# Totals over partitions on PE instead of POOL, and the tail's bias row added by PE

## The reference

```python
x = x + L0_xattn(layernorm(x), ctx)   # causal self attention + cross attention, 16 heads of 16
x = x + L0_ffn(layernorm(x))          # per-token int8 input, weights rounded to -1, 0, 1
x = x + L1_xattn(layernorm(x), ctx)   # cross attention
x = x + L1_ffn(layernorm(x))          # one int8 scale for the whole tensor

def weight_quant(w):                  # L0_ffn: sum over the whole weight
    scale = 1.0 / clip(mean(abs(w)), 1e-5)
    return clip(round(w * scale), -1, 1) / scale

def quant_per_tensor(x):              # L1_ffn: maximum over the whole tensor
    scale = maximum(max(abs(x)), 1e-6) / 127
    return round(x / scale), scale

def qlinear(x, w, b):                 # L1_ffn, twice, with gelu between
    xq, sx = quant_per_tensor(x); wq, sw = quant_per_tensor(w)
    return (xq @ wq.T + b) * (sw * sx)
```

## Time and profile before

| | |
|---|---|
| median of three runs | 2048.04 us |
| the profiled execution | 2049.73 us |
| its span, first to last instruction | 2047.9 us |
| mean granted TensorE clock | 0.911 |
| PE busy | 1735.0 us (85%) |
| DVE busy | 1348.7 us (66%) |
| ACT busy | 1168.0 us (57%) |
| POOL busy | 739.7 us (36%) |
| POOL's partition reduces | 6 |

### The profile page before, as it was taken

How to read it: one execution, slowest core, us unless ns; L and a number is a source line. 1 busy time by engine, 2 the same in 40 slices (tenths; PEclk the granted TensorE clock), 3 DMA queues, 4 the chain that set the end, 5 groups by cost and what they waited for, 6 DMA issues and landing times.

```text
span 2047.9 us, 34236 instructions
## 1 busy us (share of the span) xinstructions
PE 1735.0 (85%) x10004; PEld 745.0 (36%) x10016; DVE 1348.7 (66%) x2478; ACT 1168.0 (57%) x2178; POOL 739.7 (36%) x984
## 2 busy tenths in 40 slices
PE   5897889987999889987999799987999798777676
PEld 1243334422443244432543244332442243231225
DVE  6567666777667666757677756766677757617378
ACT  1364475566655485556655585557555675552486
POOL 3322525541544126521544136521544042150034
PEclk7798889998999989987999999988999899786898
DMA  7224313232232313331232313222331223005023
GB/s 204 81 77 122 83 32 89 78 90 62 64 104 59 94 48 85 87 81 52 68 100 70 83 48 102 74 77 59 90 87 55 65 56 101 1 26 161 23 81 103
DMA packets 106988, 159.93 MB, mean 78 GB/s; under 512 B 20657, under 2 KB 83249, under 8 KB 106801
## 3 DMA queue, kind: packets, MB, share of 16 engines
q1 hardware_dynamic: 101904, 156.43, 27.7%
q10 hardware_dynamic: 4896, 1.18, 0.3%
HBM read 105.00 MB, written 51.38 MB: 76 GB/s over the span
## 4 chain that ended last, share of the span: by engine, by line
PE 56%; DVE 14%; issue 11%; ACT 8%; POOL 7%; DMA 2%; SPq 1%; ACTq 1%; DVEq 0%; POOLq 0%
PE acc L1390 13%; PE mx L1355 12%; PE st L1376 10%; DVE nmax L1176 8%; PE misc L1330 6%; PE misc L1302 3%; PE misc L1342 3%; PE misc L1417 3%; ACT probs L931 2%; PE misc L1444 2%; POOL qk L823 1%; DMA stack<-parts_fk 1%; POOL parts L825 1%; POOL parts L821 1%; POOL parts L827 1%
## 5 line engine op out<-in xcount | busy, mean ns | idle before, releaser
L1176 DVE TENSOR_REDUCE nmax<-mx 128x1 f32<-128x512 f32 (+2 forms) x1376 | 881.4, 674 | 458.0 <-PE mx L1355 276.7
L931 ACT ACTIVATE probs<-st 128x512 f32<-128x512 f32 (+3 forms) x1536 | 773.7, 548 | 516.1 <-PE st L1376 346.4
L1355 PE MATMUL mx<-stack 96*128 96x512 bf16 (+3 forms) x1536 | 574.3, 385 | 128.7 <-DVE nmax L1176 80.6
L1376 PE MATMUL st<-stack 99*128 99x512 bf16 (+3 forms) x1536 | 565.8, 378 | 68.6 <-ACT probs L931 57.6
L1376 PEld LDWEIGHTS st<-stack 99*128 99x128 bf16 x1536 | 152.0, 100 | 443.9 <-ACT probs L931 262.2
L1355 PEld LDWEIGHTS mx<-stack 96*128 96x128 bf16 x1536 | 154.6, 101 | 342.9 <-DVE nmax L1176 237.4
L821 POOL TENSOR_TENSOR parts<-qk,zero 128x512 bf16<-128x512 f32 x94 | 98.1, 1043 | 302.5 <-ACT qk L914 302.5
L833 POOL TENSOR_TENSOR nparts<-nmax,zero 128x16 bf16<-128x16 f32 x96 | 21.1, 220 | 405.4 <-DVE nmax L1176 398.2
L1390 PE MATMUL acc<-probs,v_x 128*32 128x512 f32 x1024 | 151.0, 665 | 0.0
L1390 PE MATMUL acc<-probs,v_f 128*32 128x512 f32 x1024 | 147.4, 650 | 0.4 <-ACT probs L931 0.3
L1379 PE MATMUL st<-mask_st,identb 128*128 128x128 bf16 x512 | 112.2, 222 | 0.0
(11 more groups left out here) (231 smaller groups left out, 2051.5 us busy)
## 6 DMA issues: line engine op xcount, KB each, us to landing
parts_xk<-parts SPq DMA_DIRECT2D x48, 128.0 KB
parts_xq<-parts SPq DMA_DIRECT2D x48, 128.0 KB
stack<-parts_xq SPq DMA_DIRECT2D x32, 192.0 KB, 3.1
stack<-parts_xk SPq DMA_DIRECT2D x32, 192.0 KB, 3.7
parts_sk<-parts SPq DMA_DIRECT2D x48, 128.0 KB
parts_sq<-parts SPq DMA_DIRECT2D x48, 128.0 KB
stack<-parts_sq SPq DMA_DIRECT2D x32, 192.0 KB, 2.9
stack<-parts_sk SPq DMA_DIRECT2D x32, 192.0 KB, 3.5
```

What stands on the lines that cost most here:

```text
L931: act.activation(probs[:, j % P_SLOTS, c, T - w:], st_bank(n, 4 * j + c)[:, 0:w], ACT.Exp, scale=SCALE).then_inc(exp_done, 1)
L1176: dve.tensor_reduce(nmax[:, ring, first:first + NT * (len(cs) - 1) + 1:NT], src, AX.X, ALU.max, negate=True).then_inc(mx_free, 1)
L1355: last = pe.matmul(o, stack[0:ROWS, r, 0, c, P * i:P * i + P], stack[0:ROWS, r, 1, c, 0:w], start=True, stop=not causal)
L1376: last = pe.matmul(o[:, 0:w], stack[0:AUG, r, 1, c, P * j:P * j + P], stack[0:AUG, r, 0, c, T - w:T], start=True, stop=not causal)
```

## The change

The six `partition_all_reduce` of POOL go. For n = 0 and 1 PE multiplies wsum with a 128 x 128 view of a column of ones, which leaves the sum in every partition (`w_tot`). For the four maxima PE transposes the column into a row of one partition (`w_row`; in the tail `t_tot` and `t_htot`), DVE reduces the row to one number, and PE multiplies it with a row of ones (`to_all`); DVE reads the total from PSUM. In the order of steps the empty card and `w_scale` become `w_tot`, and for n = 2 and 3 two more cards come in, so the later cards of that list move by up to one or two places. PE now waits for DVE's `w_sum` in its own order at these steps.

In the tail POOL no longer adds G2. PE opens each of its four accumulations of a batch with an f32 matmul of the row of ones against the unscaled row G2 (256 columns), and hscale1 scales it together with the product; DVE's `sums` waits for the residual's load itself. L1242 goes, and ACT starts at `t_hsc` 3 instead of 4. After its last quantising POOL does nothing. One memset (`ones1`) is new at the start. Left out of the diff below are declarations, semaphores and the tables of steps.

```diff
@@ -216,7 +214,7 @@
-            [("w_peak", n), None, None, ("w_scale", n), ("w_ints", n, 0), None, ("w_ints", n, 1), None, ("w_ints", n, 2)] +
+            [("w_peak", n), None] + [("w_row", n), None] * (n >= 2) + [("w_tot", n), None, ("w_ints", n, 0), None, ("w_ints", n, 1), None, ("w_ints", n, 2)] +
@@ -256,7 +254,7 @@
-    "misc": {"weights": 1, "ctx_T": 1, "norm_T": 2, "project": 1, "v": 2, "negmax_T": 1, "heads_out": 1,
+    "misc": {"weights": 1, "w_row": 1, "w_tot": 1, "ctx_T": 1, "norm_T": 2, "project": 1, "v": 2, "negmax_T": 1, "heads_out": 1,
@@ -748,6 +746,7 @@
+            pool.memset(ones1[:, :], 1.0).then_inc(consts_made, 1)
@@ -768,11 +767,6 @@
-            def w_peak(s):
-                n = s.b.base
-                pool.wait_ge(w_sum, n + 1)
-                pool.partition_all_reduce(wtot[:, n, :], wsum[:, n, :], P, RADD if n < 2 else RMAX).then_inc(w_tot, 1)
@@ -858,12 +852,10 @@
-            pool.wait_ge(peak, 2 * B)
-            pool.partition_all_reduce(xtot[:, :], xrun[:, :], P, RMAX).then_inc(t_tot, 1)
@@ -874,13 +866,6 @@
-            pool.wait_ge(t_hsc, 1)
-            pool.partition_all_reduce(htot[:, :], hrun1[:, :], P, RMAX).then_inc(t_htot, 1)
-            pool.wait_ge(t_hsc, 5)
-            for n in range(B):
-                pool.wait_ge(t_res[n], 16)
-                add_row(tail_res[n].rearrange("p (t c) -> p t c", c=C), Bv["G2"], t_bias)
@@ -994,7 +979,7 @@
-            act.wait_ge(t_hsc, 4)
+            act.wait_ge(t_hsc, 3)
@@ -1035,15 +1020,18 @@
-            def w_scale_(s):
-                n = s.b.base
-                dve.wait_ge(w_tot, n + 1)
-                if n < 2:
-                    dve.tensor_scalar(wscale[:, n, :], wtot[:, n, :], 1.0 / (F * C), 1e-5, ALU.mult, ALU.max).then_inc(w_scale, 1)
-                else:
-                    dve.tensor_scalar(wscale[:, n, :], wtot[:, n, :], 1e-6, 1.0 / QP, ALU.max, ALU.mult).then_inc(w_scale, 1)
-                dve.wait_ge(w_scale, 2 * n + 1)
+            def w_row(s):
+                slot = misc_slot(s)
+                wait_misc_full(dve, s)
+                dve.tensor_reduce(wrow[:, :], misc[slot][0:1, 0:P], AX.X, ALU.max).then_inc(misc_free[slot], 1)
+            def w_tot(s):
+                n, slot = s.b.base, misc_slot(s)
+                wait_misc_full(dve, s)
+                limits = (1.0 / (F * C), 1e-5, ALU.mult, ALU.max) if n < 2 else (1e-6, 1.0 / QP, ALU.max, ALU.mult)
+                dve.tensor_scalar(wscale[:, n, :], misc[slot][:, 0:1], *limits).then_inc(misc_free[slot], 1)
+                wait_misc_read(dve, s)
@@ -1051,7 +1039,7 @@
-                    dve.wait_ge(w_scale, 2 * n + 2)
+                    dve.wait_ge(w_scale, n + 1)
@@ -1210,13 +1198,15 @@
-            dve.tensor_scalar(xscale[:, :], xtot[:, :], 1e-6, 1.0 / QP, ALU.max, ALU.mult).then_inc(t_sc, 1)
+            dve.tensor_reduce(trow[:, 0:1], mx[0][0:1, 0:P], AX.X, ALU.max).then_inc(t_row, 1)
+            dve.wait_ge(t_tot, 2)
+            dve.tensor_scalar(xscale[:, :], mx[1][:, 0:1], 1e-6, 1.0 / QP, ALU.max, ALU.mult).then_inc(t_sc, 1)
@@ -1234,12 +1224,13 @@
-            dve.tensor_scalar(hscale[:, :], htot[:, :], 1e-6, 1.0 / QP, ALU.max, ALU.mult).then_inc(t_hsc, 1)
+            dve.tensor_reduce(trow[:, 1:2], misc[0][0:1, 0:P], AX.X, ALU.max).then_inc(t_row, 1)
+            dve.wait_ge(t_htot, 2)
+            dve.tensor_scalar(hscale[:, :], misc[1][:, 0:1], 1e-6, 1.0 / QP, ALU.max, ALU.mult).then_inc(t_hsc, 1)
...
-            dve.tensor_scalar(Bv["G2"][:, :], Bv["G2"][:, :], hscale1[:, :], None, ALU.mult).then_inc(t_hsc, 1)
@@ -1252,7 +1243,7 @@
-                dve.wait_ge(t_bias, n + 1)
+                dve.wait_ge(t_res[n], 16)
@@ -1293,6 +1284,26 @@
+            def w_row(s):
+                pe.wait_ge(w_sum, s.b.base + 1)
+                wait_misc_free(pe, s)
+                pe.transpose(misc[misc_slot(s)][0:1, 0:P], wsum[:, s.b.base, :], ident[:, :]).then_inc(misc_full, 1)
+            def w_tot(s):
+                n, o = s.b.base, misc[misc_slot(s)][:, 0:1]
+                if n < 2:
+                    pe.wait_ge(w_sum, n + 1)
+                    wait_misc_free(pe, s)
+                    pe.matmul(o, ones1[:, :].to_broadcast([P, P]), wsum[:, n, :], start=True, stop=True).then_inc(misc_full, 1)
+                else:
+                    wait_misc(pe, s, 0, [misc_read(s, 0, ("w_row", n))])
+                    to_all(o, wrow[:, :]).then_inc(misc_full, 1)
+            def to_all(o, value):
+                return pe.matmul(o, ones1[0:1, :].to_broadcast([1, P]), value, start=True, stop=True)
@@ -1480,11 +1491,16 @@
+                        o = out_pairs[n % 2][h][:, C * t:C * t + C]
+                        pe.matmul(o, ones1[0:1, :].to_broadcast([1, P]), Bv["G2"][0:1, :], start=True, stop=False)
...
-                            last = pe.matmul(out_pairs[n % 2][h][:, C * t:C * t + C], tail_hq[:, n % 2, f, first:first + P],
-                                             w2T[:, f, :], start=f == 0, stop=f == KF - 1)
+                            last = pe.matmul(o, tail_hq[:, n % 2, f, first:first + P], w2T[:, f, :], start=False, stop=f == KF - 1)
...
+            pe.wait_ge(peak, 2 * B)
+            pe.transpose(mx[0][0:1, 0:P], xrun[:, :], ident[:, :]).then_inc(t_tot, 1)
+            pe.wait_ge(t_row, 1)
+            to_all(mx[1][:, 0:1], trow[:, 0:1]).then_inc(t_tot, 1)
@@ -1494,6 +1510,10 @@
+            pe.wait_ge(t_hsc, 1)
+            pe.transpose(misc[0][0:1, 0:P], hrun1[:, :], ident[:, :]).then_inc(t_htot, 1)
+            pe.wait_ge(t_row, 2)
+            to_all(misc[1][:, 0:1], trow[:, 1:2]).then_inc(t_htot, 1)
```

More of the change, by code:

```diff
@@ L33 @@
 AX = mybir.AxisListType
-RMAX = bass.bass_isa.ReduceOp.max
-RADD = bass.bass_isa.ReduceOp.add
 P = 128
@@ L420, in two_layers_kernel @@
         wsum = sb("wsum", [P, 4, 1])
-        wtot = sb("wtot", [P, 4, 1])
+        wrow, trow, ones1 = sb("wrow", [1, 1]), sb("trow", [1, 2]), sb("ones1", [P, 1])
         wscale = sb("wscale", [P, 4, 1])
         winv = sb("winv", [P, 4, 1])
-        xpeak, xrun, xtot, xscale, xinv = (sb(n, [P, 1]) for n in ("xpeak", "xrun", "xtot", "xscale", "xinv"))
-        hscale1, hrun1, htot, hscale, hinv, oscale = (sb(n, [P, 1]) for n in ("hscale1", "hrun1", "htot", "hscale", "hinv", "oscale"))
+        xpeak, xrun, xscale, xinv = (sb(n, [P, 1]) for n in ("xpeak", "xrun", "xscale", "xinv"))
+        hscale1, hrun1, hscale, hinv, oscale = (sb(n, [P, 1]) for n in ("hscale1", "hrun1", "hscale", "hinv", "oscale"))
         hpeak = sb("hpeak", [P, B // 2 * KF])
@@ L466, in two_layers_kernel @@
         NFIRST = 6
-        NMADE = 12
+        NMADE = 13
         consts_in, consts_made = sem("consts_in"), sem("consts_made")
@@ L493, in two_layers_kernel @@
         peak, stored = sem("peak"), sem("stored")
-        w_in, w_sum, w_tot, w_scale, w_quant, w_kept = \
-            (sem("ffn_w_" + n) for n in ("in", "sum", "tot", "scale", "quant", "kept"))
+        w_in, w_sum, w_scale, w_quant, w_kept = \
+            (sem("ffn_w_" + n) for n in ("in", "sum", "scale", "quant", "kept"))
         zeroed, waited = sem("zeroed"), sem("waited")
@@ L591, in two_layers_kernel @@
         t_turn, t_turned, t_peak, t_mag, t_round = sem("t_turn"), sem("t_turned"), sem("t_peak"), sem("t_mag"), sem("t_round")
-        t_out, t_sum, t_bias = sem("t_out"), sem("t_sum"), sem("t_bias")
-        t_hsc, t_htot, t_end = sem("t_hsc"), sem("t_htot"), sem("t_end")
+        t_out, t_sum = sem("t_out"), sem("t_sum")
+        t_row, t_hsc, t_htot, t_end = sem("t_row"), sem("t_hsc"), sem("t_htot"), sem("t_end")
         def st_bank(n, k):
@@ L859, in down_q @@
                 pool.tensor_tensor(hq[:, t % 2, :], hid[:, t, :], magic[:, :].to_broadcast([P, F]), ALU.subtract).then_inc(hq_full, 1)
-            walk(pool, dict(consts_rest=consts_rest, w_peak=w_peak, stats=stats_, norm=norm, mid_bias=mid_bias, project=project, negmax=negmax,
+            walk(pool, dict(consts_rest=consts_rest, stats=stats_, norm=norm, mid_bias=mid_bias, project=project, negmax=negmax,
                             y_T=y_T, hid_scale=hid_scale, down_q=down_q))
-            pool.wait_ge(peak, 2 * B)
-            pool.partition_all_reduce(xtot[:, :], xrun[:, :], P, RMAX).then_inc(t_tot, 1)
             pool.wait_ge(t_sc, 2)
@@ L1211, in finish @@
                 dve.tensor_tensor(xrun[:, :], xrun[:, :], xpeak[:, :], ALU.max).then_inc(peak, 1)
-            walk(dve, dict(consts=consts, consts_rest=consts_rest, project=project, w_peak=w_peak, w_scale=w_scale_, w_ints=w_ints, stats=stats_, norm=norm, x_scale=x_scale, quant_x=quant_x, hidden=hidden,
+            walk(dve, dict(consts=consts, consts_rest=consts_rest, project=project, w_peak=w_peak, w_row=w_row, w_tot=w_tot, w_ints=w_ints, stats=stats_, norm=norm, x_scale=x_scale, quant_x=quant_x, hidden=hidden,
                            hid_peak=hid_peak, hid_scale=hid_scale, down=down, v=v, maxima=maxima, heads_out=heads_out,
@@ L1445, in down @@
                 last.then_inc(misc_full, 1)
```

(2 more changed lines are left out.)

## The result

The changed kernel takes 2088.23 us (median of four runs, 2083.99 to 2089.55) against 2048.57 for the kernel before in the same session: ratio 1.0187, 95% interval 1.0169 to 1.0205. It is slower by 40 us, where 10.5 us less was forecast. The profiled execution took 2087.48, its span is 2085.4, so 37.5 more than the span before.

What follows compares the result with a forecast made beforehand. PE, busy 85% of the span, bounds the kernel through the batch loop, which the change leaves alone. Terms -16.0 - 2.5 + 6.0 + 0.4 + 1.6 = -10.5 us gave 2037.6 us, range 2029 to 2046.

Steps and rivals of the forecast that it cites:

- Last pass: Tail's final pass: bias matmuls make PE the bound at 5.51 us a batch, +1.6 us.
- rival C: Last pass: PE's clock does not come up; slower by over 4 us, all eight batches give +30; chance 0.08.
- First turn: First turn of the walk: removing four POOL reduces and their silent times, less added waits, gives -16 us.
- my four units: The four first-turn units that turn a weight into integers: together -21 us before added waits.
- x1: First unit with a weight in the first turn: from 25.05 to 17 us, -8.
- x2: Second unit with a weight in the first turn: down to 14.5 us, -5.9.
- s1: Third unit with a weight in the first turn: down to 15.5 us, -4.
- s2: Fourth unit with a weight in the first turn: down to 18 us, -3.
- those for the DMA: First turn: weights' loads lose cover, so DVE waits for them; +2.2 us.
- rival B: First turn: PE's waits for DVE's sums replace the stall; gain only 6, total -0.5 us; chance 0.15.
- Hand-over: Walk to tail: total over PE comes sooner, -2.5 us; POOL beside DVE stretches DVE's four instructions, +6.
- The step from hrun to hscale: In the tail: the reduce cost DVE only 0.55 us, the chain over PE 0.95; +0.4.

Runs made afterwards that it cites:

- the entry warm: Changed kernel plus 18 unused bf16 matmuls of 512 columns ahead of the last pass, so PE enters at full clock: 2041.13 us, pass 61.6.
- the run with the first turn alone: Kernel before with the totals of the four weights by PE, tail unchanged: 2033.32 us against 2050.16, ratio 0.993.
- the run with the hand-over alone: Kernel before with only the maximum over x taken across partitions by PE instead of POOL: 2048.85 us in one run.
- the waiting POOL: Changed kernel with a 128-row bf16 bias, POOL quantising batch 2 only after DVE rounded batches 0 and 1: 2023.99 us against 2050.16, ratio 0.987.
- the bias edited: Kernel before with the bias by PE as a one-row f32 matmul, no add_row, all six reduces still on POOL: 2109.73 us, pass 104.6.

## Why the prediction was wrong, step by step

**Last pass: the step that failed.** I wrote that "PE needs 3.67 + 1.84 = 5.51 a batch", with both durations read at clock 1.00, and let the low clock cost "a little" in the first batch. That the clock comes up was an assumption, taken from a pass in which it did. The engine's mixture was what the change altered. I gave rival C, where it stays low, only 0.08, because "now PE has none" of the idle times: but it was not idleness that kept the clock down here, since PE has none in 94 us. What did was the one-row matmuls: without them, or with 64 or 128 rows in their place, the clock rises. Two errors add up:

- The clock: 104.5 us against 61.6 with the entry warm, 43 of the 51 us.
- The price of a one-row matmul. I read 0.46 from a form with 128 rows, and 128 rows cost 0.43 here. One row costs 0.73 at full clock, and so do 64: before their weight loads PE's load queue stands idle at full clock too (26 loads with 64 rows: 2.7 us in all, "issue"), where before those of 128 rows it hardly does (30 loads: 0.2). A batch takes 6.42 (4 x 1.605) instead of 5.51: the biases 2.92 instead of 1.84, the products 3.50 instead of 3.67. That is 7.3 us over the eight, and the pass with the warm entry is 7.9 longer than the one before. So even with the clock up the change would have won only about 17.0 - 2.8 - 0.9 - 7.9 = 5 us.

Rival C had "all eight give +30", or 32 by its own terms (the first batch already held 1.6 of the low clock's cost); the median is +40. I had priced the eight batches at 5.51 + 5.5 = 11.0 us each; they take 11.9, since the one-row matmul costs 1.15 and not 0.92 at the low clock.

What the Trainium skill says, "TensorE: Matmul & The Clock Gate", Part 1, is that activity releases the throttle and that the clock follows how busy PE has been. By PE's busy time that would give the forecast's pass. This case disagrees as long as busy is read from the profile (59.00 of 59.00 us at 0.50). In the passes above that start at the low clock, what goes with a clock that stays there is PE's time in one-row matmuls, not its busy time. Why, no run shows, nor why the same mixture, entered at full clock, stays at it.

**First turn: near in sum, wrong in two of its four units.** Forecast 17, 14.5, 15.5 and 18 us for the units with weights, measured 17.5, 14.2, 17.4 and 21.7: -7.6, -6.2, -2.2 and +0.8, in all -15.2; my four units made -21, and the waits took it to -16. Ahead of the first unit 1.1 us are lost (86.97 against 85.85), and at the heads copy one unit later (219.13, now 204.69) the gain is 14.4. At xrun it is 17.0: the other 2.6 us come from the walk behind it, which the change leaves alone, and are luck. The run with the first turn alone gives -17.0 at xrun too, and by the ratio -14 (-18 to -11). In x1 and x2 it came as forecast, at clocks of 0.99 and 1.00; there POOL's silence was the cause. In s1 and s2 it did not: the clock stayed at 0.80 and 0.84, where I expected over 0.95. In s1 a direct wait of 4.1 us is gone, and the unit is only 2.2 shorter; PE now waits 1.7 us there for DVE's sum. In s2 there was little to win: DVE waited for POOL only 0.4 us before, and now PE waits 2.1 us for DVE's sum. The lines for s2, from the waits, first of before (181.51 to 202.38), then of after (166.68 to 188.33):

```profile
DVE wscale L1045 <- POOL wtot L774: 0.4, 1, 0.4
```

```profile
PE misc L1290 <- DVE wsum L1020: 2.1, 1, 2.1
...
DVE wsum L1020 <- DMA hid<-in_L_ffn_w_dram: 0.5, 1, 0.5
```

The waits that I had charged at 0.7 each, 2.8 in all, are 1.8, 0.4, 1.7 and 2.1, 6.0 in all; those for the DMA, charged at 2.2, are 0.5. That is rival B's mechanism, at a part of its size.

**Hand-over: right in its mechanism, both terms too large.** POOL and DVE alternate, one instruction each, and DVE's last of four ends 7.9 us after xinv (forecast 9.1, before 3.1). I had said that no row showed a tensor_scalar on POOL beside such a round; now one does: it blocks as well, and is blocked (1.55 us on both engines, instead of 0.75 on DVE and 1.10 on POOL). The rule of the Trainium skill in "SBUF — State Buffer", "Who interferes with whom", that whichever instruction starts first holds the port pair for its whole length, holds here. The chain over PE took 1.41 us instead of 0.95, 0.28 of it because a matmul of one column against one row takes 0.58 and not 0.3, 0.10 from the transpose (0.37 and not 0.27), the rest from the reduce and the hand-overs. So -2.5 was -2.05 and +6 was +4.8. Forecast +3.5, measured +2.8, the two misses taking each other off in part; the run with the hand-over alone gives the same +2.8, and that with the waiting POOL -4.8 against it. The step from hrun to hscale was mis-sized by the same chain: +0.9 instead of +0.4.

**What stays open.** The walk's end moves between kernels with the same walk: xrun at 1938.2 in the kernel before, 1933.9 with the hand-over edited, 1947.2 with the bias edited (9.5 us of that from POOL's late start); with PE's totals from 1911.3 to 1927.3 in eleven traces. Most of it lies behind the first turn: from the heads copy at 219.13 in the kernel before (204.69 after) to xrun, which no edit touches, the fourteen traces take between 1708.0 and 1719.5 us. I didn't find what sets it. At that heads copy the eleven stand at 202.7 to 208.1, the two others without the late start at 217.8 and 219.1: the first turn's gain is sure, its size 10 to 16 us. No other verdict above rests on it.

How much time in one-row matmuls keeps the clock down wasn't measured either: one in bf16 per group doesn't, one in f32 with 64 columns only delays the rise, six in bf16 do, and so does one in f32 with 256 columns. Each of these passes is one execution, but for the changed kernel: its four runs have mean clocks of 0.894 to 0.900 and times within 6 us, so as far as these tell, its pass ran at the low clock in all four.

## What to carry to other kernels

A matmul that replaces work of another engine has to be priced in its own shape and at the clock that its stage will have, and if it is narrow in rows it may decide that clock. A constant row, if it may be rounded to bf16, is added for 0.12 us a group by a full 128-row bf16 matmul (ones against the row divided by 128), where the one-row f32 form cost 51 us in this kernel. When an engine that was silent by accident becomes free, look at which transfers and ports it had left alone: one wait, on the instructions that it now disturbs, gave 4.8 us.

## What the runs showed of the hardware

- PE 100% busy for 94 us at a granted clock of 0.50, with 1.15 us of each 2.97 in one-row matmuls; the same instructions at 1.00 from first to last once the clock was up before them.
- The same f32 matmul of 256 columns adds 0.43 us at full clock to a group with 128 rows and 0.73 with 64 rows or one; a bf16 one adds 0.12 with 128 rows and 0.32 with one.
- A POOL tensor_scalar and a DVE tensor_scalar of 1024 columns, both from SBUF to SBUF, take turns: 1.55 us on each where they meet, instead of 1.10 on POOL and 0.75 on DVE.
